# Switched attention on one core: the weights are loaded and split inside the attention's own block

## The reference

```python
gate_v = _get_sel_gate(x, sel_v_w, rs)      # per position and head: 2 of 8 experts
gate_o = _get_sel_gate(x, sel_o_w, rs)
q = jnp.einsum('bsd,hpd->bhsp', x, q_w.reshape(H, P, D))
k = jnp.einsum('bsd,hpd->bhsp', x, k_w.reshape(H, P, D))
xv = jnp.einsum('bsd,hedp->bshep', x, v_w.reshape(H, E, D, P))
v = jnp.einsum('bshep,bshe->bhsp', xv, gate_v)
att = jax.nn.softmax(jnp.einsum('bhqp,bhkp->bhqk', q, k) * SCALE, axis=-1)
ctx = jnp.einsum('bhqk,bhkp->bqhp', att, v)
weighted = ctx[:, :, :, None, :] * gate_o[..., None]
out = jnp.einsum('bshep,hepd->bsd', weighted, o_w.reshape(H, E, P, D))
```

## Time and profile before

| | |
|---|---|
| median of 3 runs | 3300.31 us |
| lowest, highest | 3300.05, 3302.07 us |
| the profiled execution | 3297.7 us |
| its span, first to last instruction | 3295.9 us |
| TensorE clock granted, mean | 0.923 |
| busy: PE, DVE, ACT, POOL | 89%, 85%, 71%, 70% |
| `prepare_switch` block | 1326.65 to 1366.83 us |
| iterations 3 and 4 of the attention | 1405.5 to 1435.0, 1435.0 to 1464.7 us |

### The profile page before, as it was taken

How to read it: one execution, slowest core, us unless ns; L and a number is a source line. 1 busy time by engine, 2 the same in 40 slices (tenths; PEclk the granted TensorE clock), 3 DMA queues, 4 the chain that set the end, 5 groups by cost and what they waited for, 6 DMA issues and landing times.

```text
span 3295.9 us, 78554 instructions
## 1 busy us (share of the span) xinstructions
PE 2947.3 (89%) x24633; PEld 2207.1 (67%) x24646; DVE 2792.6 (85%) x9096; ACT 2344.1 (71%) x7533; POOL 2305.8 (70%) x3108
## 2 busy tenths in 40 slices
PE   6639997289668999399999999999999999999998
PEld 6526775167345777277777777777777777777776
DVE  4369997599897998588999989898989999898987
ACT  3276665777896666477777777777777777777776
POOL 1179996564686665167777777777777777777777
PEclk8559998599678999699999999999999999999999
DMA  3000000022000100400000000000000000000000
GB/s 111 15 12 16 16 17 7 21 73 71 1 1 21 31 29 27 124 8 8 7 9 9 8 7 9 9 8 9 7 8 9 7 7 8 9 8 7 8 8 5
DMA packets 132959, 63.73 MB, mean 19 GB/s; under 512 B 20417, under 2 KB 132161, under 8 KB 132545
## 3 DMA queue, kind: packets, MB, share of 16 engines
q1 hardware_dynamic: 132544, 58.70, 6.4%
HBM read 41.82 MB, written 8.45 MB: 15 GB/s over the span
## 4 chain that ended last, share of the span: by engine, by line
PE 57%; POOL 0%; DVE 0%; ACT 0%; issue 0%; DMA 0%; POOLq 0%; SPq 0%; DVEq 0%; ACTq 0%
PE ps_sw_a L2127 23%; PE ps_sw_d L2127 22%; PE ps_sw_w L2169 4%; PE ps_sw_w L2156 3%; PE ps_sw_s L2142 2%; PE ps_sw_s L2180 2%; PE ps_sw_m L2147 1%; PE ps_sw_m L2135 0%; ACT sw_scaled L1915 0%; POOL sw_o_rest L1881 0%; POOL sw_o_rest L1878 0%; DVE sw_v_part L2029 0%; ACT sw_probs L1964 0%; DMA sw_x<-scratch_x 0%; DVE sw_r_sel L2044 0%
## 5 line engine op out<-in xcount | busy, mean ns | idle before, releaser
L1915 ACT ACTIVATE sw_scaled<-ps_sw_a,sw_gate_o 128x128 f32<-128x128 f32 x2048 | 620.5, 447 | 252.3 <-PE ps_sw_a L2127 244.3
L1915 ACT ACTIVATE sw_scaled<-ps_sw_a,sw_gate_v 128x128 f32<-128x128 f32 x2048 | 597.7, 450 | 203.3 <-PE ps_sw_a L2127 203.2
L2029 DVE SCALAR_TENSOR_TENSOR sw_o_part<-ps_sw_d,sw_gate_o,sw_o_part 128x128 f32<-128x128 f32 x1920 | 555.1, 338 | 60.6 <-PE ps_sw_d L2127 59.5
L1854 POOL TENSOR_TENSOR sw_v_pair<-sw_v_part,sw_scaled 128x256 f32<-128x256 f32 x512 | 378.2, 739 | 158.8 <-DVE sw_v_part L2029 101.7
L2029 DVE SCALAR_TENSOR_TENSOR sw_v_part<-ps_sw_d,sw_gate_v,sw_scaled 128x128 f32<-128x128 f32 x1024 | 304.8, 338 | 123.1 <-PE ps_sw_d L2127 104.3
L1878 POOL TENSOR_TENSOR sw_o_rest<-sw_o_rest,sw_scaled 128x256 f32<-128x256 f32 x384 | 285.3, 743 | 155.2 <-ACT sw_scaled L1915 117.9
L2029 DVE SCALAR_TENSOR_TENSOR sw_v_part<-ps_sw_d,sw_gate_v,sw_v_part 128x128 f32<-128x128 f32 x1024 | 304.5, 338 | 0.0
L1881 POOL TENSOR_TENSOR sw_o_rest<-sw_o_rest,sw_scaled 128x256 f32<-128x256 f32 x384 | 282.7, 736 | 30.1
L1859 POOL TENSOR_TENSOR sw_v<-sw_v_pair 128x128 f32<-128x128 f32 x512 | 241.7, 472 | 40.1
L985 POOL TENSOR_TENSOR at_key_wide<-at_keyT,c_half_heads 128x1024 f32<-128x1024 f32 x128 | 242.5, 1895 | 4.2 <-ACT at_keyT L1082 4.2
L2127 PE MATMUL ps_sw_a<-sw_v_high,sw_xT_high 128*128 128x512 f32 x512 | 235.6, 460 | 0.4 <-ACT sw_scaled L1915 0.3
(11 more groups left out here) (326 smaller groups left out, 8582.1 us busy)
## 6 DMA issues: line engine op xcount, KB each, us to landing
at_ctxT<-ctx_T SPq DMA_DIRECT2D x128, 64.0 KB, 1.8
re_values<-in_ctx SPq DMA_DIRECT2D x128, 64.0 KB, 2.4
x<-in_x SPq DMA_DIRECT2D x16, 256.0 KB, 3.4
l_ctx<-in_ctx SPq DMA_DIRECT2D x16, 256.0 KB, 3.0
re_ctx<-in_ctx SPq DMA_DIRECT2D x16, 256.0 KB, 3.1
scratch_x<-x SPq DMA_DIRECT2D x64, 64.0 KB, 1.8
swp_staged<-in_L_ffn_v_w SPq DMA_DIRECT2D x8, 512.0 KB, 5.9
swp_staged<-in_L_ffn_o_w SPq DMA_DIRECT2D x8, 512.0 KB, 7.1
```

The source lines that it names most:

```text
L1854: pool.tensor_tensor(v_pair[:, h % 2], v_part[:, h], scaled[:, h % 4, 2:4], ALU.add)\
L1915: act.activation(scaled[:, h % 4, e], ps_a[h % 2][:, e], ACT.Copy, scale=gates[:, s, h, HALF_E + e:HALF_E + e + 1]).then_inc(a_scaled[kind ...
L2029: dve.scalar_tensor_tensor(out=acc[:, e % 2], in0=ps_d[h % 2][:, e], scalar=gates[:, s, h, e:e + 1], in1=before, op0=ALU.mult, op1=ALU.add ...
```

## The change

The block `prepare_switch` is gone, and its work is written into the queues of the attention's block. No buffer of its own holds the raw weights: the key and query weights land in `scaled`, the selection weights in `y`, the eight v pieces (512 KB each) take turns in five places (two halves of `v_part`, `v`, two halves of `scaled`), and the o weights come as sixteen half pieces (256 KB each) in four places (`o_part`, `o_pair`, `o_rest` and a new `spare`).

- SP issues the two key/query loads, three small loads, `place`, x of tiles 0 and 1, and v pieces 0 to 2 without a wait; piece 3 waits for the pair products (which read `scaled`), pieces 5 to 7 for the low parts of pieces 0 to 2. Then o half pieces 0 to 3, and 4 to 15 in iterations 2 and 3, each waiting for the low part of the one four before.
- ACT rounds all eight v pieces at the end of iteration 1, behind tile 0's exponentials, and one o half piece behind the scaling of each v unit in iterations 2 and 3. Its first scaling waits for the low parts of v pieces 4 and 7.
- DVE makes the low parts of v pieces 0, 2, 3, 5 and 7 at the end of iteration 1 and of an o half piece behind the mix of each v unit in iterations 2 and 3; it also keeps the pair products behind tile 0's `norm`. POOL makes the low parts of v pieces 1, 4 and 6 at the end of its iteration 1.
- PE turns the selection weights and makes the pair products ahead of its loop, and each unit of tile 0 waits for its own low parts.

The core of the diff:

```diff
-    W = prepare_switch(k, A, C)
+    W = {}
...
+        raw_v = [v_part[:, 0:4].rearrange("p h b d -> p (h b) d"), v_part[:, 4:8].rearrange("p h b d -> p (h b) d"), v[:],
+                 scaled[:, 0:2].rearrange("p a e d -> p (a e) d"), scaled[:, 2:4].rearrange("p a e d -> p (a e) d")]
+        raw_o = [o_part[:].rearrange("p a b d -> p (a b) d"), o_pair[:].rearrange("p a b d -> p (a b) d"), o_rest[:],
+                 spare[:]]
+        prep = k.sems("sw_prep", "keys", "small", "pair_ps", "sel_ps", "kept", "route")
+        raw_in = {n: [k.sem(f"sw_raw_in_{n}{h}") for h in range(len(raw))] for n, raw in (("v", raw_v), ("o", raw_o))}
+        high = {n: k.sem("sw_high_" + n) for n in "vo"}
+        low = {n: k.sem("sw_low_" + n) for n in "vo"}
+        low_pool = k.sem("sw_low_pool")
+
+        def o_half(w, p):
+            return w[:, p // 2, p % 2 * HALF_E:(p % 2 + 1) * HALF_E]
+
+        def low_v_done(h):
+            if h in POOL_SPLITS:
+                return low_pool, POOL_SPLITS.index(h) + 1
+            return low["v"], h + 1 - sum(p < h for p in POOL_SPLITS)
+
+        def only_first(step):
+            def at(i, s, rd):
+                if i == 0:
+                    step()
+            return at
...
             def _(sp):
+                for n, m in enumerate(("q_w", "k_w")):
+                    sp.dma_start(raw_pair[:, n], A[f"L3_ffn_{m}"].rearrange("(h p) d -> p h d", p=P)).then_inc(prep["keys"], 16)
+                for n, m in enumerate(("sel_v_w", "sel_o_w")):
+                    sp.dma_start(raw_sel[n * S:(n + 1) * S], A[f"L3_ffn_{m}"]).then_inc(prep["small"], 16)
+                sp.dma_start(route_scale[:], on_all(A["L3_ffn_route_scale"], 1)).then_inc(prep["small"], 16)
...
                 def tile_in(dst, i):
...
                 def store(i, s, rd):
...
-                straight([(0, fetch), (2, fetch_residual), (4, store)])
+
+                def fetch_v():
+                    for h in range(SH):
+                        if h == 3:
+                            sp.wait_ge(prep["pair_ps"], 1)
+                        if h >= 5:
+                            sp.wait_ge(*low_v_done(h - 5))
+                        src = A["L3_ffn_v_w"][h * SE:(h + 1) * SE].rearrange("e i o -> i e o")
+                        sp.dma_start(raw_v[h % 5], src).then_inc(raw_in["v"][h % 5], 16)
+
+                def fetch_o(lo, hi):
+                    def step():
+                        for p in range(lo, hi):
+                            if p >= 4:
+                                sp.wait_ge(low["o"], p - 3)
+                            src = A["L3_ffn_o_w"][p * HALF_E:(p + 1) * HALF_E].rearrange("e i o -> i e o")
+                            sp.dma_start(raw_o[p % 4], src).then_inc(raw_in["o"][p % 4], 16)
+                    return step
+                straight([(0, fetch), (1, only_first(fetch_v)), (1, only_first(fetch_o(0, 4))), (2, fetch_residual),
+                          (2, only_first(fetch_o(4, 10))), (3, only_first(fetch_o(10, 16))), (4, store)])
...
                         if h == 1:
-                            if not first(i, 1):
+                            if i == 0:
+                                pool.wait_ge(low["o"], 2 * SH)
+                            else:
...
+
+                def low_v(h):
+                    def step():
+                        pool.wait_ge(high["v"], h + 1)
+                        pool.tensor_tensor(W["v"]["low"][:, h], raw_v[h % 5], W["v"]["high"][:, h].bitcast(F32), ALU.subtract)\
+                            .then_inc(low_pool, 1)
+                    return only_first(step)
...
-                straight(stages)
+                straight(stages + [(1, low_v(h)) for h in POOL_SPLITS])
...
             def _(act):
...
                     def step(i, s, rd):
...
+                        if i == 0 and h == 0 and kind == "v":
+                            act.wait_ge(*low_v_done(4))
+                            act.wait_ge(*low_v_done(7))
                         if h == 0:
...
+
+                def round_v(h):
+                    def step():
+                        act.wait_ge(raw_in["v"][h % 5], 16 * (h // 5) + 16)
+                        act.activation(W["v"]["high"][:, h], raw_v[h % 5], ACT.Copy).then_inc(high["v"], 1)
+                    return only_first(step)
+
+                def round_o(p):
+                    def step():
+                        act.wait_ge(raw_in["o"][p % 4], 16 * (p // 4) + 16)
+                        act.activation(o_half(W["o"]["high"], p), raw_o[p % 4], ACT.Copy).then_inc(high["o"], 1)
+                    return only_first(step)
...
-                straight(stages)
+                stages = [step for st in stages for step in
+                          ([st, (2, round_o(vs.index(st))), (3, round_o(SH + vs.index(st)))] if st in vs else [st])]
+                straight(stages + [(1, round_v(h)) for h in range(SH)])
...
             def _(dve):
...
+                dve.wait_ge(prep["small"], 48)
+                ones = C["ones"][:, 0:SH]
+                dve.tensor_scalar(W["route"][:, 0], ones, route_scale[:], None, ALU.mult).then_inc(prep["route"], 1)
+                dve.tensor_scalar(W["route"][:, 1], ones, route_scale[:], C["gates"][:, 7:8], ALU.mult, ALU.mult)\
+                    .then_inc(prep["route"], 1)
+                dve.wait_ge(prep["sel_ps"], 1)
+                dve.tensor_copy(W["sel"][:], ps_m[:, 1]).then_inc(prep["kept"], 1)
+
+                def keep_pairs():
+                    dve.wait_ge(prep["pair_ps"], 1)
+                    for n in range(2):
+                        dve.tensor_copy(W["pair"][:, 4 * n:4 * n + 4], ps_w[n].rearrange("p (h t) -> p h t", h=4))\
+                            .then_inc(prep["kept"], 1)
+
+                def low_v(h):
+                    def step():
+                        dve.wait_ge(high["v"], h + 1)
+                        dve.tensor_tensor(W["v"]["low"][:, h], raw_v[h % 5], W["v"]["high"][:, h].bitcast(F32), ALU.subtract)\
+                            .then_inc(low["v"], 1)
+                    return only_first(step)
+
+                def low_o(p):
+                    def step():
+                        dve.wait_ge(high["o"], p + 1)
+                        dve.tensor_tensor(o_half(W["o"]["low"], p), raw_o[p % 4], o_half(W["o"]["high"], p).bitcast(F32),
+                                          ALU.subtract).then_inc(low["o"], 1)
+                    return only_first(step)
...
                 def wide(ap):
...
                         if n == 0:
...
+                        elif n == ROUTED and i == 0:
+                            dve.wait_ge(prep["route"], 2)
+                            dve.wait_ge(q["ranked"], RANK * i + n)
...
-                stages = [(1, norm)]
+                stages = [(1, norm), (1, only_first(keep_pairs))]
...
+                        if kind == "v" and n % 2:
+                            stages += [(2, low_o(n // 2)), (3, low_o(SH + n // 2))]
+                stages += [(1, low_v(h)) for h in range(SH) if h not in POOL_SPLITS]
...
                     def step(i, s, rd):
...
-                        ready = []
+                        ready = [low_v_done(h) if kind == "v" else (low["o"], 2 * h + 2)] if i == 0 else []
                         if h == 0:
-                            ready = [(q["xT_low"], i + 1)] if kind == "v" else [(q["ctx_low"], 2 * i + 2)]
+                            ready.append((q["xT_low"], i + 1) if kind == "v" else (q["ctx_low"], 2 * i + 2))
...
                 def logits(i, s, rd):
+                    if i == 0:
+                        pe.wait_ge(prep["kept"], 1)
...
                 def pair_keys(n):
                     def step(i, s, rd):
-                        if not first(i, 2):
+                        if i == 0:
+                            pe.wait_ge(prep["kept"], 2 + n)
+                        elif not first(i, 2):
...
-                        elif i == 1:
+                        else:
...
+                pe.wait_ge(prep["small"], 48)
+                pe.transpose(ps_m[:, 1], raw_sel, C["ident"][:]).then_inc(prep["sel_ps"], 1)
+                pe.wait_ge(prep["keys"], 32)
+                for h in range(SH):
+                    m = pe.matmul(ps_w[h // 4][:, h % 4 * P:(h % 4 + 1) * P], raw_pair[:, 1, h], raw_pair[:, 0, h],
+                                  start=True, stop=True)
+                m.then_inc(prep["pair_ps"], 1)
...
```

More of the change, by code:

```diff
@@ L1664 @@
 HALF_E = SE // 2
[L1665 to L1704, removed]
-                for h in range(SH):
-                    m = pe.matmul(ps[h // 4][:, h % 4], raw[:, 1, h], raw[:, 0, h], start=True, stop=True)
-                m.then_inc(q["pair_ps"], 1)
-                pe.transpose(ps_sel, sel[:], C["ident"][:]).then_inc(q["sel_ps"], 1)
-            @block.scalar
-            def _(act):
-                act.preload_act_table(ACT.Exp)
-                for h in range(SH):
-                    act.wait_ge(weights_in[h], 32)
```

(35 more changed lines are left out.)

## The result

The kernel after takes 3282.8 us (median of 5 runs, 3280.2 to 3284.2) beside 3300.3 for the kernel before: 0.9947 of it, with a 95% interval of 0.9936 to 0.9958. The forecast was 3291.1 with a range from 3285.5 to 3297.5: the sign was right, the gain is 17.5 us instead of 9.2.

A forecast was written before the change was run, and what follows sets the result against it. Bytes loaded were taken to bound the head, TensorE the steady state. Head -19.5, iteration 2 +6.1 and iteration 3 +4.2 sum to -9.2 us, from 3300.3 to 3291.1, range 3285.5 to 3297.5.

The forecast's parts named there:

- The change touches nothing there: Attention's steady state: TensorE stays busy through a tile's 29.7 us, and only the state's beginning shifts.
- The head: First DMA to ACT's first scaling: o's bytes leave the path and tile 0's start overlaps v's loading, 19.5 us saved.
- Tile 0's turn: PE's turn for tile 0 at the start: 33.1 us earlier, some 11 us behind the attention's first DMA.
- the empty queue: Landing of the last v piece in the head: 4.4 us for 512 KB with no other transfers queued.
- Iteration 2: Tile 0's v units: low parts 3.4, hold-ups 1.4 and PE's clock 1.3 add 6.1 us.
- The low clock at the start: Iteration 2: PE, after a pause without work, runs its first two units at the lower level, costing 1.3 us.
- The low parts: Iteration 2: DVE's seven o low parts cost 3.4 us after waits, plus 1.4 for hold-ups beside POOL.
- Iteration 3: Tile 1's v and tile 0's o units: DVE's low parts 2.6 and hold-ups 1.6 add 4.2 us.
- Edits at nothing: O half-piece fetches, SP's queue order, tile 1's norm and PE's waits for tile 0's low parts cost nothing.
- The additions hide: Iterations 2 and 3: new DVE work goes into existing hold-ups, gain about 16 us, 3284 us; chance 0.10.
- Full hold-ups: Iterations 2 and 3: each low part waits out a POOL addition, 0.52 us; gain 4.4, 3296 us; chance 0.20.
- late half pieces: Iterations 2 and 3: o half pieces land late and ACT waits; 3304 us at a 13 us landing; chance 0.06.

The follow-up runs named there:

- pad_after_all: Kernel after plus an unused 32-byte buffer ahead of the layer norm's buffers, putting matmul operands back at the kernel before's addresses modulo 64; 0.9970 of the kernel before.
- no_o: Kernel after without loading, rounding and splitting the o weights, o units using v's weights instead; 3270.5 us, 0.9908 of the kernel before.

## Why the prediction was wrong

- **What bounds it, and that the steady state is untouched: wrong.** "The change touches nothing there" took the steady state's instructions for its time. The change allocates buffers ahead of the matmuls' operands. Undoing that alone (pad_after_all) gives 0.9970, a gain of 9.9 us (6.3 to 13.2); the forecast was 9.2. The missing 7 us, and all by which the range was missed, are this term, which the prediction put at nothing.
- **The head: -19.5.** It was -21.2 in the two profiles compared, and -20.6 between the means of all profiles with the same work there (55.7 in the kernel before and its three padded forms, 35.1 in the kernel after, twice, and its three padded forms). Tile 0's turn came 9.90 us behind the first DMA, not 11.3, and ACT was free 10.85 us behind it, not 11.17: 1.7 us. From there to the first scaling it was 13.69, forecast 13.6, from terms that missed in both directions: piece 7 was fetched 5.7 us later (forecast 5.9), its landing took 5.3 (4.4, the empty queue), and the tail behind it 2.7 (3.2). GpSimd's 2.33 us were 2.34 alone (the last piece) and 2.47 and 2.96 with DVE.
- **Iteration 2: +6.1.** +4.9 in the compared profiles, +5.7 between means (29.0 and 23.3). The sum came out, in part by luck, for its terms were other ones. To the end of the last v mix the forecast had 6 us more, and it was 4.1 and 5.3 in the two profiles of the kernel after (19.06 and 20.29 us, before 14.98). The low clock at the start, forecast 1.3, cost 2.5 in no_o (17.45 there), which got 1.0 back by its faster context. The low parts, forecast 4.8 with their hold-ups, came on top with 2.7 to the last mix, because DVE already waited 3.4 us for PE there in no_o and this wait took them in part. The rest, 0.7 us ahead of the context, had no term. A low part took 0.66 to 0.72 us on average, and it was POOL that waited: its `sw_v_pair` rose from 733 to 991 ns.

```profile
L1841 POOL TENSOR_TENSOR sw_v_pair<-sw_v_part,sw_scaled 128x256 f32<-128x256 f32 x16 | 15.9, 991 | 14.7 <-DVE sw_v_part L2069 8.4 <-ACT sw_scaled L1914 6.0
```

- **Iteration 3: +4.2.** +2.8 and, between means, +3.4 (32.8 and 29.4); 4.0 by no_o. DVE took over as the bound, as said.
- **Edits at nothing: right, but for the steady state.** ACT waits for no DMA in iterations 2 and 3. DVE's mixes still waited for PE in iteration 2, 0.4 us in the first profile and 1.7 in the second, where it was 0.8 before; in iteration 3 they didn't in these two.
- **Rivals.** "The additions hide" named 3284 us, which is close, for a reason that is false: both iterations did cost. Full hold-ups (3296 us) and late half pieces are out. The forecast's own sum came out at 3290 with the operands where they were, by a head that was 1 us too small and an iteration 2 with the wrong terms, and then a term was missing in it.

## What to carry to other kernels

Here a change that added buffers moved every buffer allocated behind them. Where TensorE sets the pace of a long loop, compare the operands' addresses before believing that the loop is untouched, and give an experiment the same addresses as its base. Low parts shared out between VectorE and GpSimd at the same time took longer than on VectorE alone: time the pair, not the single operation. And compare profiles from a mark at the stage that changed, since the stages ahead varied by 15 us here.

## What the runs showed of the hardware

- A 128x512 fp32r matmul with a 128x128 stationary operand started every 228.5 to 230.0 ns in the mean where both operands lay at the same address modulo 64 (32 and 32, or 0 and 0), and every 232.9 to 233.5 ns where one lay at 0 and the other at 32. Why isn't shown; other offsets weren't tried.
- A load of 512 KB, the third in a row, landed in 5.9 to 6.1 us (four profiles) where its place in SBUF began at 0 modulo 64 and in 6.7 to 7.1 us (five) where it began at 32; other buffers had moved with it, so the cause isn't shown.
- A VectorE subtraction of 128x1024 with two SBUF inputs took 1.22 us alone and 2.66 and 3.40 us beside the same operation on GpSimd, which took 2.34 us alone and up to 2.96: two pieces shared out took 3.55 and 4.04 us, one after the other on VectorE 2.35.
- The clock of TensorE came back to its upper level 3.8 to 6.6 us behind the same instruction in profiles of kernels with the same work there, and at 3.8 and 6.6 in two profiles of one kernel; iteration 2 was 1 us longer where it came late.
- The 32 matmuls of the context took 3.68 us at the lower clock level throughout, and 2.50 us where the clock fell 1.3 us into them.
